# First mamba batch's gate on VectorE, second norm in four groups, last gate in four steps between GpSimd's driving products

## What is computed

```python
xn = layernorm(x)
s  = attention(xn)                 # softmax over theta(q k^T), 512 x 512 per batch, then Wo
g  = silu(xn + moe(layernorm(xn))) # 8 experts, top 1, and a shared expert
x  = x + s * g                     # first gate
xn = layernorm(x)                  # second norm
xv = silu(conv(xn @ W_in)); dt, B, C = split(xv @ W_x)
delta = softplus(dt @ W_dt + b_dt)
h_t = exp(delta*A) * h_(t-1) + delta*B*xv   # 16 states, scan over 512 rows
s  = (sum_n h*C + xv*D) @ W_out
x  = x + s * silu(ffn(xn))         # quantised weights
```

## Time and profile before

| what | us |
|---|---|
| three timed runs, median (lowest, highest) | 776.02 (774.17, 777.29) |
| the profiled execution | 773.97 |
| its span | 772.1 |
| attention of batches 3 to 7 | 203 to 329 |
| first scan to first scan, first round | 67.4 |
| the same, a steady round | 53.1 |

### The profile page before, as it was taken

How to read it: one execution, slowest core, us unless ns; L and a number is a source line. 1 busy time by engine, 2 the same in 40 slices (tenths; PEclk the granted TensorE clock), 3 DMA queues, 4 the chain that set the end, 5 groups by cost and what they waited for, 6 DMA issues and landing times. The chain is left out here.

```text
span 772.1 us, 12626 instructions
## 1 busy us (share of the span) xinstructions
PE 658.4 (85%) x3975; PEld 488.8 (63%) x3975; DVE 645.7 (84%) x1086; ACT 501.5 (65%) x1019; POOL 534.5 (69%) x337
## 2 busy tenths in 40 slices
PE   1897979998958988767799998998998999988685
PEld 0874655554535545545677776876887777767665
DVE  5878856665768676668989999999999999999998
ACT  0564644443644577467868879879788787797453
POOL 1005734455553121677788899999999999999996
PEclk9999999999988999989899999999999999999999
DMA  7901132221421140024505514625336136246000
GB/s 195 288 1 35 49 108 65 70 67 48 56 27 14 14 166 1 27 83 114 133 1 166 146 38 133 151 84 129 105 112 157 49 122 167 58 136 151 1 2 27
DMA packets 43056, 67.50 MB, mean 87 GB/s; under 512 B 6264, under 2 KB 30208, under 8 KB 42992
## 3 DMA queue, kind: packets, MB, share of 16 engines
q1 hardware_dynamic: 31744, 48.35, 19.9%
q0 software_dynamic: 9520, 17.78, 11.3%
q10 hardware_dynamic: 1728, 0.57, 0.3%
HBM read 46.01 MB, written 9.67 MB: 72 GB/s over the span
## 5 line engine op out<-in xcount | busy, mean ns | idle before, releaser
L1838 DVE TENSOR_TENSOR_SCAN xnT_all<-psum,nfT_all 128x1024 f32<-128x1024 f32 x128 | 288.9, 2276 | 6.0 <-issue 5.8
L1322 PEld LDWEIGHTS psum<-W_out,xnT_all 128*128 128x128 f32 x2048 | 237.8, 193 | 60.6 <-issue 58.0
L1322 PE MATMUL psum<-W_out,xnT_all 128*128 128x128 f32 x2048 | 243.4, 278 | 32.1 <-DVE work L1854 30.0
L1538 ACT ACTIVATE psum<-delta,A 128x511 f32<-128x511 f32 x256 | 165.1, 683 | 68.0 <-DVE xnT_all L1838 67.9
L1302 POOL TENSOR_TENSOR nfT_all<-attn_all,du 128x1024 f32<-128x1024 f32 x64 | 158.6, 2627 | 2.4 <-DVE xnT_all L1838 2.4
L1302 POOL TENSOR_TENSOR nfT_all<-nf_rows,du 128x1024 f32<-128x1024 f32 x63 | 147.4, 2361 | 6.6 <-DVE nfT_all L1992 3.8
L1854 DVE SCALAR_TENSOR_TENSOR work<-psum,Cc,work 128x128 f32<-128x128 f32 x300 | 82.2, 338 | 7.1 <-PE psum L1322 7.1
L811 POOL DMA_INDIRECT xs_dram<-nf_rows,pos x32 | 33.1, 1033 | 58.4 <-DVE pos L1001 49.0
L823 POOL DMA_INDIRECT moe_dram<-nf_rows x39 | 37.8, 969 | 47.9 <-ACT nf_rows L947 47.9
L1197 POOL TENSOR_TENSOR du<-du,res_all 128x512 f32<-128x512 f32 x8 | 10.9, 1365 | 79.4 <-ACT du L1547 79.4
L1322 PE MATMUL psum<-vo_all,W_taps 128*128 128x512 f32 (+3 forms) x128 | 58.8, 604 | 0.0
(11 more groups left out here) (224 smaller groups left out, 1168.0 us busy)
## 6 DMA issues: line engine op xcount, KB each, us to landing
nf_rows<-bt_dram SPq DMA_DIRECT2D x32, 512.0 KB, 4.3
attn_all<-bt_dram SPq DMA_DIRECT2D x32, 512.0 KB, 4.3
delta<-rl POOLq DMA_DIRECT2D x7, 512.0 KB, 7.0
e<-ab POOLq DMA_DIRECT2D x7, 512.0 KB, 7.4
delta<-e POOLq DMA_DIRECT2D x7, 512.0 KB, 6.1
xs_dram<-attn_all SPq DMA_DIRECT2D x4, 645.0 KB, 8.7
nf_rows<-xs_dram SPq DMA_DIRECT2D x39, 64.5 KB, 1.9
x_all<-in_x_dram SPq DMA_DIRECT2D x8, 256.0 KB, 5.8
```

What stands on the lines that cost most here:

```text
L1322: return nc.tensor.matmul(o, l, r, start=start, stop=stop)
L1538: ins = nc.scalar.activation(dA[:, i % RA, k, 1:L], delta[:, p, h, 1:L], ACT.Exp, scale=A[:, h, 2 * q + k:2 * q + k + 1])
L1838: nc.vector.tensor_tensor_scan(hring[:, i % R, :, :].rearrange("p n l -> p (n l)"), dA[:, i % RA, :, :].rearrange("p n l -> p (n l)"), dbx ...
```

## The change

Group 3 to 7 of the second norm is cut in two, 3 to 6 and 7. Batch 0's gate becomes three VectorE operations at (3, 2), with its tanh on ScalarE moved from (3, 1) to (3, 0); GpSimd starts with batch 1 and waits for x1 first. The root of group 0 moves from (4, 0) to (3, 3), the norm from (4, 1) to (4, 0). The tanhs of batches 5 and 6 move one place earlier, to (6, 3) and (7, 0); the statistics of batch 4 move to (6, 3), those of batch 5 out of the first scan round to (7, 1). In the scans, the moments of group 2 stand behind the second scan of the first round, those of group 3 behind the additions of the second round's second pair; their roots follow the logarithm of the round. The last gate's four steps stand ahead of the products of q = 2 to 5. In the diff the four steps of `gated` are left out; they are as before, each under its condition.

```diff
@@ -1109,7 +1109,7 @@
...
             ow = late(10).rearrange("p (j d) -> p j d", d=D)
-            GROUPS = ((0,), (1, 2), (3, 4, 5, 6, 7))
+            GROUPS = ((0,), (1, 2), (3, 4, 5, 6), (7,))
@@ -1188,26 +1188,32 @@
...
 
-                def gated(i):
+                def gated(i, steps=(0, 1, 2, 3)):
...
                     g = gt[:, i % 2, :]
...
+                    if 0 in steps:
...
+                    if 1 in steps:
...
+                    if 2 in steps:
...
+                    if 3 in steps:
...
                 for i in range(NB - 1):
-                    gated(i)
+                    if i:
+                        pool.wait_ge(F["x1"], i)
+                        gated(i)
@@ -1272,8 +1278,8 @@
...
                         for q in range(NP):
-                            if q == 1 and not end:
-                                gated(NB - 1)
+                            if 2 <= q < 6 and not end:
+                                gated(NB - 1, (q - 2,))
@@ -1553,7 +1559,7 @@
...
                 def norm_later(i):
-                    act.wait_ge(F["rs"], len(GROUPS) + 1)
+                    act.wait_ge(F["rs"], 4 if i in GROUPS[2] else 6)
@@ -1673,8 +1679,6 @@
...
                             ffn_tanh(q - 2)
-                        if q == 3 and not end:
-                            roots(2)
@@ -1693,6 +1697,8 @@
...
                             ln_one_plus()
+                            if b < 2:
+                                roots(b + 2)
@@ -1714,12 +1720,14 @@
...
 
-                    if (b, s) == (FIRST, 1):
+                    if (b, s) == (FIRST, 0):
                         gates(0)
+                    elif (b, s) == (FIRST, 1):
                         gates(1)
+                    elif (b, s) == (FIRST, 3):
+                        roots(0)
...
                         gates(2)
-                        roots(0)
@@ -1737,11 +1745,12 @@
...
                     elif (b, s) == (FIRST + 3, 3):
+                        gates(5)
...
                     elif (b, s) == (FIRST + 4, 0):
-                        gates(5)
+                        gates(6)
@@ -1749,7 +1758,6 @@
...
                     elif (b, s) == (FIRST + 4, 1):
-                        gates(6)
@@ -1804,7 +1812,7 @@
...
                     nc.vector.reciprocal(rs1[:, c], std1[:, c]).then_inc(F["rs"], 1)
-                    dve.wait_ge(F["rs"], g + 1)
+                    dve.wait_ge(F["rs"], 2 * g - 1)
@@ -1926,16 +1934,28 @@
...
                                     add_state(b, p, m)
-                        if q == 1 and not end:
-                            statistics(NB - 3)
+                        if q == 0 and b == 0:
                             statistics(NB - 2)
-                        if q == 2 and not end:
+                            moments(2)
+                        if q == 1 and b == 1:
                             statistics(NB - 1)
-                            moments(2)
-                        if q == 3 and not end:
-                            shifts(2)
+                            moments(3)
+                        if q == 3 and b < 2:
+                            shifts(b + 2)
...
                             gate()
+
+                def first_gated():
+                    def rows_of(a):
+                        return a[:, 0:TPB, :].rearrange("p j d -> p (j d)")
+
+                    g = gt[:, 0, :]
+                    dve.wait_ge(F["si"], 1)
+                    nc.vector.scalar_tensor_tensor(g, g, 1.0, rows_of(res_all), ALU.add, ALU.mult).then_inc(F["gs"], 2)
+                    dve.wait_ge(F["gs"], 2)
+                    nc.vector.tensor_tensor(g, g, rows_of(attn_all), ALU.mult).then_inc(F["sg"], 1)
+                    dve.wait_ge(F["sg"], 1)
+                    nc.vector.tensor_tensor(rows_of(x_all), rows_of(x_all), g, ALU.add).then_inc(F["x1"], 1)
@@ -1949,11 +1969,13 @@
...
 
-                    if (b, s) == (FIRST, 3):
+                    if (b, s) == (FIRST, 2):
+                        first_gated()
+                    elif (b, s) == (FIRST, 3):
...
                         moments(0)
-                    elif (b, s) == (FIRST + 1, 1):
+                    elif (b, s) == (FIRST + 1, 0):
@@ -1967,8 +1989,10 @@
...
                         norms(1)
-                    elif (b, s) == (FIRST + 4, 0):
+                    elif (b, s) == (FIRST + 3, 3):
                         statistics(4)
+                    elif (b, s) == (FIRST + 4, 1):
+                        statistics(5)
...
```

More of the change, by code:

```diff
@@ L1195, in gated @@
                     g = gt[:, i % 2, :]
-                    pool.wait_ge(F["si"], i + 1)
-                    nc.gpsimd.tensor_tensor(g, g, rows_of(res_all), ALU.mult).then_inc(F["gs"], 1)
-                    pool.wait_ge(F["gs"], 2 * i + 1)
-                    nc.gpsimd.tensor_tensor(g, g, rows_of(res_all), ALU.add).then_inc(F["gs"], 1)
-                    pool.wait_ge(F["gs"], 2 * i + 2)
-                    pool.wait_ge(S["attn"], at(i, "attn", 1))
-                    nc.gpsimd.tensor_tensor(g, g, rows_of(attn_all), ALU.mult).then_inc(F["sg"], 1)
-                    pool.wait_ge(F["sg"], i + 1)
-                    nc.gpsimd.tensor_tensor(rows_of(x_all), rows_of(x_all), g, ALU.add).then_inc(F["x1"], 1)
+                    if 0 in steps:
+                        pool.wait_ge(F["si"], i + 1)
+                        nc.gpsimd.tensor_tensor(g, g, rows_of(res_all), ALU.mult).then_inc(F["gs"], 1)
+                    if 1 in steps:
+                        pool.wait_ge(F["gs"], 2 * i + 1)
+                        nc.gpsimd.tensor_tensor(g, g, rows_of(res_all), ALU.add).then_inc(F["gs"], 1)
+                    if 2 in steps:
+                        pool.wait_ge(F["gs"], 2 * i + 2)
+                        pool.wait_ge(S["attn"], at(i, "attn", 1))
+                        nc.gpsimd.tensor_tensor(g, g, rows_of(attn_all), ALU.mult).then_inc(F["sg"], 1)
+                    if 3 in steps:
+                        pool.wait_ge(F["sg"], i + 1)
+                        nc.gpsimd.tensor_tensor(rows_of(x_all), rows_of(x_all), g, ALU.add).then_inc(F["x1"], 1)
                 pool.wait_ge(S["res"], at(FIRST - 1, "res", 1))
```

## The result

Each ratio below is to the kernel before, run beside it. A difference in us between two changed kernels can be one between medians from different chips and times; the kernel before took 775.85 to 776.45 us in each of them.

The account below looks back on a forecast made before the run. VectorE, busy 51.2 of 53.1 us, bounds steady rounds; only the attention stage and first round can shorten. 6.2 + 0.5 + 7.9 - 6.9 = 7.7 us saved from the median 776.02 gives 768 us, range 760.5 to 774.0.

Parts of the forecast that it names:

- A: Attention stage: first gate on VectorE, root and norm earlier, saves 6.2 us; bounds 4.3 and 6.9.
- the wait and the gate product at 228: Attention stage: VectorE's 6.25 us wait for the first root goes; its gate product moves from 234.26 to near 228 us.
- the earlier chain: Attention stage: up to 0.7 us more saved if the whole chain comes earlier with the variance.
- GpSimd's second gate: Attention stage: runs from about 209.3 to 214.7 us, over when the moments begin, so most of 3.5 us of stalls goes.
- B: Sixth and seventh gates one step earlier: 0.8 us gained, 0.3 lost, 0.5 net; bounds -0.6 and 0.8.
- C: First scan round: saves 7.9 us, giving a round of 59.5; bounds 1.6 and 12.8.
- the stop ahead of the third scan: First round: VectorE's 5.42 us stop goes, replaced by 4.5 us of statistics and moments; third scan stays at 340.3.
- the shift: Second operation, reading two SBUF tiles, waits for GpSimd's product: 1.4 us in the first round, 0.6 in the second.
- the 1.9 us of TensorE at the end: End of first round: TensorE's 2.43 us wait shrinks to about 0.5, its projections no longer starting late.
- D: Second scan round: the last batch's statistics, moments, shifts and root cost 6.9 us; between 2.3 and 11.6.
- rival 3: Moments and shifts, first two rounds: exclusion worse than counted; slower from 17.2 us of waits, up to 782 us; chance 0.07.
- Rival 2: Gains given to other engines: TensorE holds first round at 63 us, variance 2 us late; 774 us; chance 0.18.

Follow-up runs that it names:

- late_root: Changed kernel with the first root behind the third gate's tanh and the norm one place later again, first gate kept on VectorE: 771.82 us.
- no_first_gate: Changed kernel with the first gate back on GpSimd and the first root and norm back in their old places: 775.82 us.
- whole_last_gate: Changed kernel with the last gate's four steps together ahead of products 2 and 3 on GpSimd: 768.91 us.
- attention_alone: Changed kernel with the scans as before the change, including one group of batches 3 to 7; only the attention-stage parts kept: 765.25 us.
- the columns: Changed kernel with the shifts' second operation written column by column, as 16 and 4 VectorE operations of 128x1: 762.70 us.
- moments_gpsimd: Changed kernel with the moments of groups 2 and 3 on GpSimd as seven tiny operations, statistics and shifts still on VectorE: 765.28 us.
- both_gpsimd: Changed kernel with the moments of groups 2 and 3 and the shifts' product on GpSimd: 759.82 us.

## Why the prediction was right, step by step

*A, right in its mechanism, too small by 1.6 to 2.2 us*: 6.2 forecast, 7.8 by the traces and 8.4 by the medians with and without it. I had the wait and the gate product at 228. I gave the earlier chain at most 0.7 us, while late_root shows 2.8 (traces) to 4.0 us (medians) for the gate alone. I left out that TensorE was granted 0.50 behind the stop. And GpSimd's second gate was not over when the moments began (it ended at 216.87, 214.7 forecast), so 1.5 us of waiting stayed in them.

*B, 0.5 forecast*: the two delta operations take 1.21 and 1.23 us for 2.29 and 2.11, TensorE's turn has no wait for 0.81, and the way from the last gate product (305.07, and 296.95 after) to the first scan is 1.03 us shorter, for the 0.8 I had. What the earlier tanh costs ahead of that gate product is not in this number. From the first query scaling to the first scan no_first_gate, which has B and not A, is 0.45 us shorter than before (137.07 for 137.52): near the 0.5, in one execution of each.

*C, 7.9 forecast, 6.74 measured.* Right: the stop ahead of the third scan is only exchanged for statistics and moments, and spreading the gate steps is worth nothing there (whole_last_gate). Mis-sized: the shift, 1.4 us of waiting forecast, 2.8 measured (2.95 less the 0.18 that the same operation took in attention_alone). Wrong in its reason: the 1.9 us of TensorE at the end. I put it down to the late root; attention_alone has that root and not the wait, and no_first_gate has the wait in its second round and not that root. It goes with the granted clock (0.57 or 1.00), which the sum had nowhere, so that these 1.9 us came in is luck.

*D, -6.9 forecast, -7.92 measured.* Statistics and moments took 4.7 us (394.22 to the next scan at 398.95), 5.9 forecast; the shift and its reciprocal 2.9, 1.0 forecast. In both rounds the shift is the term that failed: I took a part of a product, and it waits for the rest of one and a whole second.

So the total came out near because errors cancelled, and that is luck. A and B together save 11.0 us by the medians (776.23 to 765.25, attention_alone), with 2.25 of them in the first scan round, where I had 6.7; C and D, which I had as a gain of 1.0, cost 2.2. The waits for GpSimd in the two rounds, each slow operation less the 0.15 to 0.18 us that it takes alone, come to 3.5 + 2.8 + 3.1 + 2.6 = 12.0 us where I had 9.5. So rival 3's mechanism was at work, over the 9.5 in my sum and short of the 17.2 from which it decides. Rival 2 was wrong of TensorE here (rounds of 54.9 are possible), but its kind appears as soon as VectorE stops waiting: GpSimd becomes late.

The Trainium skill's rule (SBUF — State Buffer, "Who interferes with whom") that two SBUF inputs on VectorE exclude GpSimd's reads, and one outside the two-port modes does not, is borne out by the columns: 2.03 us for sixteen beside a running product. It also says that whoever issues first has the pair. The shifts do not bear that out: the one at 351.41 in after began 0.20 us ahead of the second product (351.61) and still ended with it (354.36 and 354.31). The operation at 348.40 in moments_gpsimd began 0.47 us ahead of two products and ended, at 353.86, with the second (353.83). But there GpSimd was issuing a DMA from 348.22 to 349.11, which the operation may have met first: in the attention stage of after, tiny operations of 0.53 and 0.45 us ended together at 217.61, with no GpSimd operation beside them but a DMA issue from 216.82 to 218.13. No run separates the two.

## What to carry to other kernels

Moving a small VectorE operation to another place doesn't remove its wait while GpSimd is busy there; change its form to one tensor and a scalar column, or give it to GpSimd, and price a wait at up to two of GpSimd's operations. A wait removed on one engine pays only until the next engine's reserve is used up: in both_gpsimd GpSimd took back 2.8 us of what VectorE had saved. Where a sum of parts comes out right, run the parts: here the half in the scans was a small loss.

## What the runs showed that was not expected

*GpSimd's products can go ahead of a waiting VectorE operation.* In one place a tiny operation got in after the running product (0.52 us at 326.59, its end at 327.11, half-way through the two products); the next waited for a whole one (2.35), the shifts for more than one (2.95 and 2.79), in moments_gpsimd for two and what stood ahead of them (5.46).

*TensorE's clock differs between executions behind the same work.* At the start of the stage, behind the same wait of 0.37 us, the granted clock from 188 to 196 us was 1.00 in the execution of before and 0.79 in that of after, and the first query products took 1.12 and 2.07 us. Before, then after:

```profile
188.00:196.00 8.00, 6.05 (x19) 2.82 (x18) 1.80 (x3) 3.04 (x7) 4.37 (x4) 1.00 0.10 28
```

```profile
188.00:196.00 8.00, 6.05 (x16) 2.65 (x16) 1.27 (x3) 1.24 (x3) 4.29 (x5) 0.79 0.08 26
```

Later, with the same queue in after and in attention_alone and gaps of 1.33 and 1.94 us in both, the stretches from 268 to 276 us were granted 1.00 in after, and 0.75 and 0.82 in attention_alone, where VectorE's next stop ahead of a gate product was 2.98 us for 1.54. After, then attention_alone:

```profile
268.00:272.00 4.00, 2.06 (x14) 1.42 (x13) 4.00 (x10) 3.24 (x6) 1.68 (x2) 1.00 0.89 274
272.00:276.00 4.00, 4.00 (x18) 2.31 (x18) 2.35 (x5) 2.67 (x7) 0.00 (x0) 1.00 1.03 377
```

```profile
268.00:272.00 4.00, 2.06 (x8) 1.39 (x8) 3.97 (x9) 2.78 (x6) 1.15 (x1) 0.75 0.92 335
272.00:276.00 4.00, 4.00 (x15) 2.41 (x14) 1.53 (x3) 1.84 (x6) 0.00 (x0) 0.82 1.00 406
```

What decides between them in one execution stays open.
